# Identity products in TensorE's idle time, and a projected tile that waits for less

## The reference

```python
# layer 0 attention: 16 heads of 8, on normalised x
scores = jnp.einsum('bqhd,bkhd->bhqk', q, k) / d ** 0.5
attn = jax.nn.softmax(scores, axis=-1)
Y = jnp.einsum('bhqk,bkhd->bqhd', attn, v).reshape(b, n, d)
return Y @ Wo.T + bo
# layer 0 feed-forward: each token goes to the one expert with the largest gate
# layer 1 attention: the same with a relative position bias, and causal
att = att + rel_bias
att = jnp.where(causal, att, -jnp.inf)
att = jax.nn.softmax(att, axis=-1)
y = jnp.einsum('bhts,bhsd->bhtd', att, v)
return y.transpose(0, 2, 1, 3).reshape(B, T, C) @ W_proj + b_proj
```

## Time and profile before

| what | value |
|---|---|
| median of 3 runs | 1034.49 us (1031.09 to 1035.31) |
| profiled execution, its own time | 1036.33 us |
| its span in the trace | 1034.5 us |
| TensorE busy | 899.6 us, 87% |
| VectorE busy | 805.0 us, 78% |
| ScalarE busy | 612.7 us, 59% |
| GpSimd busy | 199.8 us, 19% |
| mean granted clock of TensorE | 0.921 |

### The profile page before, as it was taken

How to read it: one execution, slowest core, us unless ns; L and a number is a source line. 1 busy time by engine, 2 the same in 40 slices (tenths; PEclk the granted TensorE clock), 3 DMA queues, 4 the chain that set the end, 5 groups by cost and what they waited for, 6 DMA issues and landing times. The chain is left out here.

```text
span 1034.5 us, 22166 instructions
## 1 busy us (share of the span) xinstructions
PE 899.6 (87%) x8501; PEld 458.8 (44%) x8501; DVE 805.0 (78%) x1600; ACT 612.7 (59%) x1280; POOL 199.8 (19%) x249
## 2 busy tenths in 40 slices
PE   5589999999899987984689999999998898777788
PEld 3212222222222223883345445555535666645568
DVE  7789999999899861656787787778862587799687
ACT  3228888888888786543236677766754346433552
POOL 2202033331302110540200011103010023133221
PEclk9659999999999898996779999999969998988899
DMA  2632435524426321111645753334301000000001
GB/s 77 186 87 61 118 95 124 101 70 94 99 76 146 96 60 19 50 35 49 177 99 141 188 104 87 88 73 88 68 7 30 6 1 2 1 0 1 4 6 36
DMA packets 62678, 73.71 MB, mean 71 GB/s; under 512 B 21144, under 2 KB 46865, under 8 KB 62559
## 3 DMA queue, kind: packets, MB, share of 16 engines
q1 hardware_dynamic: 48222, 49.23, 19.8%
q0 software_dynamic: 8576, 17.86, 7.2%
q10 hardware_dynamic: 5776, 5.22, 1.6%
HBM read 44.59 MB, written 18.16 MB: 61 GB/s over the span
## 5 line engine op out<-in xcount | busy, mean ns | idle before, releaser
L1025 DVE TENSOR_REDUCE a_negmax<-a_mbank 128x1 f32<-128x1024 f32 (+4 forms) x640 | 488.3, 818 | 72.7 <-PE a_mbank L829 35.2
L982 ACT ACTIVATE a_probs<-a_ebank 128x512 f32<-128x512 f32 (+3 forms) x896 | 436.3, 554 | 163.6 <-PE a_ebank L859 85.5
L850 PE MATMUL a_ebank<-b_moving,b_still 50*128 50x512 bf16 (+4 forms) x1280 | 270.0, 368 | 19.4 <-ACT a_probs L982 10.6
L821 PE MATMUL a_mbank<-a_moving,a_still 48*128 48x512 bf16 (+4 forms) x1280 | 263.3, 377 | 22.5 <-DVE a_negmax L989 9.8
L873 PE MATMUL a_acc<-a_probs,a_slot_v 128*32 128x512 f32 (+3 forms) x1792 | 224.9, 575 | 1.1 <-ACT a_probs L982 1.1
L850 PEld LDWEIGHTS a_ebank<-b_moving,b_still 58*64 58x64 bf16 (+1 forms) x1280 | 85.0, 102 | 254.0 <-ACT a_probs L982 198.6
L821 PEld LDWEIGHTS a_mbank<-a_moving,a_still 56*64 56x64 bf16 (+1 forms) x1280 | 69.3, 104 | 89.1 <-DVE a_negmax L1025 65.5
L859 PE MATMUL a_ebank<-a_bias_b,anti 64*64 64x176 bf16 (+4 forms) x1728 | 88.3, 231 | 0.0
L859 PEld LDWEIGHTS a_ebank<-a_bias_b,anti 64*64 64x64 bf16 x1728 | 69.6, 110 | 9.0 <-issue 0.2
L829 PE MATMUL a_mbank<-bias_a,anti 64*64 64x176 bf16 (+3 forms) x576 | 65.2, 238 | 0.0
L873 PEld LDWEIGHTS a_acc<-a_probs,a_slot_v 128*32 128x32 f32 x1792 | 35.8, 109 | 52.1 <-issue 42.0
(11 more groups left out here) (388 smaller groups left out, 1118.1 us busy)
## 6 DMA issues: line engine op xcount, KB each, us to landing
a_slot_v<-vo SPq DMA_DIRECT2D x16, 512.0 KB
b_moving<-stack SPq DMA_DIRECT2D x64, 96.0 KB
b_still<-stack SPq DMA_DIRECT2D x32, 192.0 KB
a_still<-stack SPq DMA_DIRECT2D x60, 96.0 KB, 2.8
a_moving<-stack SPq DMA_DIRECT2D x60, 96.0 KB, 2.9
expert<-in_expert_rows POOLq DMA_DIRECT2D x8, 578.0 KB, 4.0
a_bias_b<-trow SPq DMA_DIRECT2D x32, 66.0 KB
b_moving<-a_mparts SPq DMA_DIRECT2D x124, 2.0 KB
```

The costliest lines, as they stand in the source:

```text
L821: last = nc.tensor.matmul(mbank[COLS * c:COLS * (c + 1), bank, lo - left:hi - left], S.a_still[rows, q % 2, pr, at[c]:at[c] + COLS], S.a_m ...
L850: last = nc.tensor.matmul(ebank[COLS * c:COLS * (c + 1), s % NE, lo:512], S.b_still[rows, buf, pr, at:at + COLS], S.b_moving[rows, buf, h, ...
L982: nc.scalar.activation(probs[:, g % 2, j, lows[g]:512], ebank[:, s % NE, lows[g]:512], ACT.Exp).then_inc(p_full, 1)
L1025: nc.vector.tensor_reduce(to[:, at:at + 1], mbank[:, (index - 1) % NM, 0:right - left], AX.X, ALU.max, negate=True).then_inc(m_empty, 2 if ...
```

## The change

A helper `keep_awake` issues `count` f32 products of the identity with some of its own columns; nothing reads the results. It is called in these places:

- at the start of TensorE's work in layer 1's front: 16 products;
- at the end of TensorE's work in each front: 26 in layer 0, ahead of the four ranking matmuls, and 32 in layer 1;
- at the last transpose of maxima of both attentions: a wait for the bank, then 5 products, then the waits and the transpose as before;
- in the second attention, ahead of each of the uses 49 to 63: one product of a quarter of the use's columns;
- in the openings, behind each use below `opening[0]`: two products of 128 columns in the first attention, one of a quarter of the use's columns in the second, into a bank of `ebank` that is not used yet;
- at the end of the experts' block: a wait and 40 products.

Apart from this, `projected(t)` waits for `t + 2` in place of `max(t + 2, NM + 1)`, and a loop variable is renamed because `n` is now the use's number.

```diff
@@ front_phase, TensorE
                 pe.wait_ge(gate_loaded, 48)
+            else:
+                keep_awake(nc, S, tp[:, 0, :], 16)
             for c in range(CHUNKS + 1):
...
                 last.then_inc(gated, 1)
+            keep_awake(nc, S, tp[:, 1, :], 26 if first else 32)
             if first:
                 pe.wait_ge(picked, 1)
@@ new function
+def keep_awake(nc, S, out, count, width=P):
+
+    for _ in range(count):
+        nc.tensor.matmul(out[:, 0:width], S.ident[:], S.ident[:, 0:width], start=True, stop=True)
@@ attention_phase, TensorE
             def transpose_maxima(n, units_done, quads_done, h):
 
+                bank = n % NM
+                if n == NQUAD * USES:
+                    pe.wait_ge(m_empty, n + 1)
+                    keep_awake(nc, S, mbank[:, bank, :], 5)
                 pe.wait_ge(m_empty, max(NM + units_done, n + 1))
                 if quads_done and causal:
                     pe.wait_ge(combined, quads_done)
-                bank = n % NM
@@ a_use
-                pe.wait_ge(m_empty, q * USES + (use + 1))
+                n = q * USES + use
+                pe.wait_ge(m_empty, n + 1)
                 left, right = unit_columns(uses[use], causal)
+                if causal and opening[3] <= n < opening[4]:
+                    keep_awake(nc, S, mbank[:, bank, :], 1, (right - left) // 4)
...
                 last.then_inc(m_full, 2 if (q, use) == (0, LATE - 1) else 1)
+                if n < opening[0]:
+                    keep_awake(nc, S, ebank[:, 1, :], 1 if causal else 2, (right - left) // 4 if causal else P)
@@ projected
-                pe.wait_ge(m_empty, NQUAD * USES + max(t + 2, NM + 1))
+                pe.wait_ge(m_empty, NQUAD * USES + (t + 2))
@@ experts' block, TensorE
             for i in range(CT, BT):
                 project(i)
+            pe.wait_ge(raw_ready, NB)
+            keep_awake(nc, S, yp[:, 0, :], 40)
```

More of the change, by code:

```diff
@@ L818, in a_use @@
                     at = [qt * P + COLS * c for c in range(P // COLS)]
-                    near = [(max(n - REACH, lo), min(n + HALF, hi)) if causal else (0, 0) for n in at]
+                    near = [(max(i - REACH, lo), min(i + HALF, hi)) if causal else (0, 0) for i in at]
                     for c, (first, end) in enumerate(near):
```

## The result

The changed kernel takes 1084.91 us (median of 4 runs, 1080.58 to 1086.49) against 1034.78 us before (4 runs): a ratio of 1.048 with a 95% interval of 1.043 to 1.052. The sign was forecast, the size was not: 50 us lost, where the forecast had 12.5 and its range ended at 1051.

What follows compares the result with a forecast made beforehand. VectorE bounded both openings; cold products would make TensorE the bound. Terms -0.6 +11.5 +0.5 -1.2 +0.4 -0.4 +0.6 +11.3 -1.9 -7.7 = +12.5 us on 1036.3, runs' median 1.8 lower: 1047 us predicted, range 1016 to 1051.

Steps and rivals of the forecast that it cites:

- Both openings cold, TensorE the bound: Both attentions' openings: clock at half, products make TensorE the bound; +11.5 and +11.3 us, chance 0.48.
- 23 x 1.73: First attention's opening: 23 uses, each 1.73 us with its two products at half clock, 39.8 us; term +11.5 us.
- 32 x 0.43: Second attention's opening: 32 products at 0.43 us at half clock, 13.8 us on TensorE; term +11.3 us.
- Uses 49 to 63: Second attention, behind its opening: the products remove the cold stretch that followed; -1.9 us (0 to -3.3).
- 15 products x 0.23 = 3.4 us, within PE's idle: Second attention, 529.5 to 539.9 us: full-clock products fit within TensorE's idle 3.1 of 10.4 us.
- Last maxima, -7.7: End of the second attention: products and shorter tile wait keep the clock up; -7.7 us (0 to -10).
- Block ends: Products at fronts and experts: layer 0's front -0.6, experts +0.4, layer 1's front start -0.4 and end +0.6 us.
- -0.4 of the 16 products: Start of layer 1's front: products cost nothing, cold matmuls at 482.15 us remain; 0 to -1.6, taken -0.4 us.
- -1.2 for the wait at 340: First attention: a shifted start may spare the wait at 340 us and its cold stretch; -1.2 us (0 to -2.5).
- Rival 1: Clock kept in both openings, products hidden behind VectorE: 1018 us, chance 0.22.
- Rival 3: First opening at full clock, second at half: 1030.5 us, chance 0.10.
- About a tenth of the slices read 5 to 7: Reading of the clock row on the profile page of the kernel before: how many slices dip.

Runs made afterwards that it cites:

- lead: Changed kernel with eight more products ahead of each attention's first use: median 1071.3 us (5 runs), ratio to before 1.033.
- same_format_fill: Kernel before plus two bf16 matmuls of 512 columns, instead of f32 products, behind each first-opening use: 1046.4 us (one run), first exponential 16.9 us late.
- second_opening_narrow: Kernel before plus one 8-column product behind each use of the second attention's opening: 1052.6 us (one run), opening 19.1 us later.
- mid_alone: Kernel before plus only the products ahead of uses 49 to 63 of the second attention: 1047.4 us (2 runs), ratio 1.016.
- no_opening: Changed kernel without the products in the two openings: median 1044.4 us (5 runs), ratio to before 1.013.
- no_opening_no_mid: Changed kernel without the products in both openings and at uses 49 to 63: median 1033.4 us (10 runs), ratio to before 1.0015.
- first_opening_alone: Kernel before plus only two products behind each use of the first attention's opening: 1051.5 us (one run), opening 21.1 us later.
- second_opening_wide: Kernel before plus products at the fronts' ends, eight ahead of each attention, and one 128-column product behind each second-opening use: 1047.7 us (one run).
- first_warm: Kernel before plus layer 0's 26 front products, five ahead of the first use, the first opening's products and the shorter tile wait: 1025.9 to 1052.4 us.

## Why the prediction was right and wrong

- **Both openings cold, TensorE the bound.** Right, with the falls where they were expected (just behind 41.5 us, and near 530). `lead` shows that the same instructions cost nothing at full clock in the first. The scores, forecast for 81 to 82 and for 533 us, began at 90.0 and 563.5: the path was right and its price wrong.
- **First opening, the term "23 x 1.73".** Mis-sized: a use takes 2.12 us, and 23 times the missing 0.39 is the 9 us between the forecast +11.5 and the measured +20.2. I added streaming times and put the passage between neighbouring matmuls at nothing. By `same_format_fill` it costs 0.41 us per use, 0.22 with a bf16 fill and 0.19 more with f32.
- **Second opening, the term "32 x 0.43".** Mis-sized by the same kind of omission: +21.6 against +11.3. From first maximum to first exponential the stage takes 37.7 us; less TensorE's own 13.8 of busy time in that stretch of the kernel before, that is 0.75 per product, not 0.43. `second_opening_narrow` shows that the streaming is the small part; what the large part is made of is argued from its weight loads, not tested.
- **Uses 49 to 63.** The sign was wrong: -1.9 forecast, +9 in the changed kernel's trace, 11 by the medians, +7.9 in `mid_alone`. The failed step is "15 products x 0.23 = 3.4 us, within PE's idle", and with it that the cold stretch behind it goes: the clock fell in all four traces with the products, for 20 us or more, and then a narrow use takes 0.91 us instead of 0.57. The stretch to be saved was itself one draw, absent from four of eleven traces.
- **Last maxima, -7.7.** The trace shows -8.0, but the term does not belong to the change: by ten runs each the parts concerned are worth nothing beyond 3.6 us either way. That the number came true in this trace is luck. Taking one profiled execution's cold stretch as the kernel's habit was the error.
- **Block ends.** The 32 products delay the second attention by 0.5 us, about the +0.6 that was forecast (0.3 for the whole front in `no_opening`). The experts' 40 cost 0.4 in `no_opening_no_mid`, as forecast, and 1.2 in the changed kernel. The -0.4 of the 16 products is not seen: from the first transpose to the last gate matmul layer 1's front takes 20.8 to 22.1 us with them (four traces) and 20.9 to 22.3 without.
- **First attention, -1.2 for the wait at 340.** In the changed kernel that place stayed at full clock, and from the first to the last exponential it took 2.7 us less. But `first_opening_alone`, which has nothing changed there, took 2.4 less: chance again.
- **Rival 1, clock kept in both: 1018 us.** Its premise can be had for the first opening, by more filling at its start, and is then worth 3.1 us rather than 5. For the second it was mispriced: with the clock kept, `second_opening_wide` still loses 8 us there, if with wider products.
- **Rival 3, first warm and second cold: 1030.5 us.** `lead` in its shorter runs is this case, and took 1065.0 to 1071.3: the terms for the second opening and the uses 49 to 63 are wrong in it as in the forecast.
- **Two readings.** "About a tenth of the slices read 5 to 7": it is six of forty. "15 products": the trace has 14, as one of the numbers 49 to 63 is a transpose of maxima. Little hangs on either, and the sums come out as written.

## What to carry to other kernels

A filler matmul is not priced by its streaming: two products of 128 columns between bf16 matmuls at half clock cost here half as much again as they stream, and one of 8 columns, which streams next to nothing, still 0.52 us. And it takes its place on TensorE's queue even where it does not keep the clock up. Fill only where the engine would stay below the other engine's pace at *half* clock, or where the stretch's start can be filled so densely that the clock does not fall there, run after run; otherwise idle time that cost nothing turns into the bound. And take what one profile shows of the clock for one draw: find the same stretch in other executions before booking its recovery as a gain.

## What the runs showed of the hardware

- The clock fell to 0.50 with no idle gap above 1.9 us nearby (1.88 and 0.76 us in the changed kernel). `first_warm` ran once in 1025.9 us, with a mean granted clock of 0.952, and three times in 1050.7 to 1052.4, with 0.919 to 0.924.
- At 1.2 GHz, passing from bf16 matmuls on 48 rows to ones on 128, or back, cost 0.11 us each time (period 1.93 us in `same_format_fill`, against an estimated 1.71 of streaming); two f32 products instead of two bf16 matmuls of equal streaming cost 0.19 us more.
- An f32 product of only 8 columns held TensorE for 0.52 us at half clock, with its two weight loads busy for 0.50; one of 128 columns for 0.73.
- From 577.6 to 597.8 us TensorE was busy for all of 20.2 us, and the granted clock stayed at 0.50.
- The same place in unchanged code ran at full clock in some traces and at half in others: 0, 7 or 17 us of half clock behind the second opening in eleven traces.
